# Two ways to apply the causal mask before a row maximum: TensorE for the wide tiles of batch 0 only, VectorE for the narrow ones

## The chip, the cores and the metric

The kernel runs on one core of a Trainium2 chip. The metric is the device time of one execution in microseconds (us); lower is better. The engines of the core are named as the profile names them: PE is TensorE (PEld its weight loads), DVE is VectorE, ACT is ScalarE, POOL is GpSimd, SP is SyncE, which here issues DMAs.

## The reference, cut to what matters

```python
x = L0_attn_x                                    # [2, 1024, 512] float32
xn = layernorm(x)
q, k, v = proj(Wq), proj(Wk), proj(Wv)           # 16 heads of 32
scores = einsum('bhqd,bhkd->bhqk', q, k) / sqrt(32)
scores = where(triu(ones((t, t)), k=1), -inf, scores)
attn = softmax(scores, axis=-1)
s = einsum('bhqk,bhkd->bhqd', attn, v) ... @ Wo.T
hidden = fwht(silu(xn @ W1.T) * (xn @ W3.T))     # 2048 wide
g = silu(hidden @ W2.T)
out = x + s * g
```

The softmax needs the maximum of each row of masked scores before the exponentials. Only that maximum, and the mask in it, is touched here.

## The kernel before

The two batches are worked one after the other. A batch has three stages: `project` (Q, K and V, each product split into high and low parts), `heads` (attention for 16 heads, with the up and gate products of the feed-forward network woven in) and `tail` (attention output, down product, gating, store). In the profiled execution the stage `heads` of batch 0 lies at about 88 to 370 us and that of batch 1 at about 567 to 842 us.

**A head in 12 slots.** `heads` counts slots g; a head has `NS` = 12 of them. In each even slot PE makes the scores of two steps (L1468), ACT takes the exponential (L828), POOL masks the diagonal block in SBUF (L664), ACT makes the high part of the probabilities (L838) and DVE the low part (L1171, called p_lo). PE multiplies them with V in groups (L1486, L1488) and fills every slot with a share of the feed-forward products (L1507), 48 matmuls a head. These masks of POOL and the products of V are not touched.

**The maxima.** Ahead of each head, during the head before it, PE computes for each of the 8 row tiles t the scores of that tile as query rows by keys (L1449), into one of two PSUM places: bank pair `M` for t of 4 to 7 (640 to 1024 columns, two matmuls) and bank `X` for t of 0 to 3 (128 to 512 columns, one matmul). The order is `MAX_ORDER = [7, 0, 5, 1, 6, 2, 4, 3]`, so the two places alternate; item r of this order waits on PE until DVE has done item r-2 (`after(pe, max_done, n * NT + r - 1)`, L1442). The slots are `MAX_AT = [-3, -2, -1, 0, 1, 3, 4, 5]`, counted from the start of the head before, so the first three fall into the last three slots of the head before that. The plan of the slots is written out by hand; no cost model places them.

**The mask in the maxima.** There are two forms, chosen by `masked_by_matmul`:

- by PE: after the scores of a tile, one more matmul (L1452) adds `causal`, -1e38 above the diagonal, to the diagonal 128 x 128 block in PSUM through an identity in bfloat16 (accumulating, `start=False`). DVE then takes a plain row maximum (`tensor_reduce`, L1156).
- by DVE: no extra matmul. DVE takes `tensor_tensor_reduce` (L1158), which adds the mask from SBUF, writes the sum back to the PSUM place and keeps the maximum. It shows as two records in the profile, CUSTOM_DVE_ANT_0 and DVE_READ_ACCUMULATOR2_ANT; the second writes the maximum to `mx`.

Before the change the heads n = 1 to 15 (batch 0 but its first head) go by PE for all 8 tiles; head 0 and all 16 heads of batch 1 go by DVE.

**What follows the maxima.** In slot 7 PE transposes the 8 maxima of the next head (L1458, into bank `X`), having waited for all of them. ACT copies the high part (L877), DVE makes the low part m_lo (L1164), SP stores both by DMA into two rows of the stacked Q tile (L514), and PE's scores of the next head wait for that DMA at their first step (`pe.wait_ge(m_in, (n + 1) * 32)`, ahead of L1468). After every second transpose in batch 0 two small matmuls (L1431) sum squares of weights.

**Order around it.** Each engine works its own list in order. In a slot DVE does first the maximum planned for the slot before, then p_lo, then the reciprocal (L1189), the gating of the feed-forward product (L1193, L1200) and m_lo. Batch 0 has work that batch 1 has not: squares of weights on ACT (L863), their scales on DVE (L1074 to L1084), and slabs of a transform on POOL (L650).

```python
def max_parts(t):
    half = (t + 1) * P // 2
    if t >= TPC:
        return M[:].rearrange("p b w -> p (b w)")[:, W - half:W + half], [(0, half), (half, 2 * half)]
    return X[:, 0, 0:(t + 1) * P], [(0, (t + 1) * P)]
...
for g in range(SLOTS + DRAIN):
    ...
    for jm, r in MAX_PLAN.get(g, []):
        maxima(n0 + jm, r)
```

Of the kernel before, what the change touches and what calls it, by code (L numbers as in the profile page):

```python
# [32 lines left out]
NH, DH = 16, 32  # L33
# [5 lines left out]
TPC = W // P  # L39
# [70 lines left out]
def build(nc, x, wq, wk, wv, wo, w1w3, w2, hadamard, out):  # L110
# [6 lines left out]
    with ctx:  # L117
# [172 lines left out]
        def after(e, s, count):  # L290

            if count > 0:
                e.wait_ge(s, count)
# [55 lines left out]
# [4 lines that stand above are left out]
                return M[:].rearrange("p b w -> p (b w)")[:, W - half:W + half], [(0, half), (half, 2 * half)]  # L353
            return X[:, 0, 0:(t + 1) * P], [(0, (t + 1) * P)]

        def masked_by_matmul(n):

            return 0 < n < NH

        def ct_bank(t):  # L360

# [11 lines left out]
        def stacks_loaded(n):  # L373

            b, j = divmod(n, NH)
            return (b * len(range(j % 3, NH, 3)) + j // 3 + 1) * STACK_LOADS
# [609 lines left out]
        def _(dve):  # L986
# [100 lines left out]
            def project(b):  # L1087
# [40 lines left out]
                for t in range(NT):  # L1128
                    heads_of = lambda v: v.rearrange("p (h d) -> p h d", h=NH)
                    for r in MAX_BEFORE.get(t, []):  # L1130
                        maxima(b * NH, r)
                    g = NQK + t
                    dve.wait_ge(proj_hi_done, b * NG + g + 1)
                    dve.tensor_tensor(vparts[:, t, :, DH:2 * DH], heads_of(group_bank(g)), vparts[:, t, :, 0:DH],
                                      ALU.subtract).then_inc(proj_lo_done, 1)
                    if b == 0 and t == 0:
                        scale_of_w13(0)
                    if t in ONES_AFTER:
                        dve.memset(k_st[ONES_AFTER.index(t)][STACK:STACK + 2, :].bitcast(F32), 1.0
                                   ).then_inc(ones_ready, 1)  # L1140
                    if t == MT_BEFORE - 1:
                        maxima_lo(b * NH)
                        if b == 0:
                            scale_of_w13(1)
                for r in range(FIRST_MAX_AT.count(None)):
                    maxima(b * NH + 1, r)

            def maxima(n, r):

                t = MAX_ORDER[r]  # L1150
                width = (t + 1) * P
                dve.wait_ge(max_ps, n * NT + r + 1)
                dve.sem_inc(max_begun, 1)
                bank, _ = max_parts(t)
                if masked_by_matmul(n):
                    dve.tensor_reduce(mx[n % 2][:, t:t + 1], bank, axis=AX.X, op=ALU.max).then_inc(max_done, 1)  # L1156
                    return
                dve.tensor_tensor_reduce(out=bank, in0=bank,  # L1158
                                         in1=causal[:, S - width:S], scale=1.0, scalar=LOWEST, op0=ALU.add,
                                         op1=ALU.max, accum_out=mx[n % 2][:, t:t + 1]).then_inc(max_done, 1)  # L1160
# [42 lines left out]
            def heads(b):  # L1203
                n0 = b * NH
                for g in range(SLOTS + DRAIN):
                    j, s = divmod(g, NS)
                    for jm, r in MAX_PLAN.get(g - 1, []):
                        maxima(n0 + jm, r)
                    if 1 <= g <= SLOTS:
                        probs_lo(n0 * NS + g - 1)  # L1210
                    if s == COPY_AT[0] and j < NH:
                        denominators(n0 + j, 0)
                    if s == COPY_AT[1] and j > 0:
                        denominators(n0 + j - 1, 1)
                    for jf, c, m in GROUP_PLAN.get(g - 1, []):
                        if m == 0:
                            gate(n0 + jf, c)
                        else:
                            hide(n0 + jf, c)
                    if g - 1 in WO_PLAN:  # L1220
                        split_wo(b, WO_PLAN[g - 1])
                    if g - 1 in MT_PLAN:
                        maxima_lo(n0 + MT_PLAN[g - 1])
                        if b == 0 and MT_PLAN[g - 1] - 1 in SUM_PLAN:
                            scale_of_w13(SUM_PLAN[MT_PLAN[g - 1] - 1])
                    if 0 <= g - SLOTS - CT_AT - 1 < 2:
                        ct_low(b, g - SLOTS - CT_AT - 1)
# [81 lines left out]
        def _(pe):  # L1309
# [21 lines left out]
            def project(b):  # L1331
# [54 lines left out]
                for g in range(2, NG):  # L1386
                    if g - NQK in MAX_BEFORE:
                        pe.wait_ge(proj_lo_done, b * NG + NQK)
                        pe.wait_ge(unscale_done, 1)
                        for r in MAX_BEFORE[g - NQK]:  # L1390
                            maxima(b * NH, r)
                    if g - NQK == MT_BEFORE:
                        transpose_maxima(b * NH)
                        if b == 0:
                            sum_of_squares(1)
                    group(g)
                    for t in XT_AFTER.get(g, ()):
                        transpose_xn(b, t)
                    if b == 0 and g == BOUND_AFTER:
                        bound_of_v()  # L1400
                    if b == 0 and g == 3 * KT:
                        transpose_v_scale()
                    if b == 0 and g == NQK:
                        pe.wait_ge(proj_lo_done, NQK - 1)
                        sum_of_squares(0)
                for r in range(FIRST_MAX_AT.count(None)):
                    maxima(b * NH + 1, r)
# [26 lines left out]
            def maxima(n, r):  # L1434

                t, q, k = MAX_ORDER[r], q_st[n % NH % 3], k_st[n % NH % 3]
                if r == 0:
                    pe.wait_ge(stack_in[n % NH % 3], stacks_loaded(n))
                if r == 1:
                    after(pe, m_lo_done, n)  # L1440
                else:
                    after(pe, max_done, n * NT + r - 1)  # L1442
                if r == 1 and n == 0:
                    pe.wait_ge(w13_scale_step, 1)
                if r == 1 and n - 2 in SUM_PLAN:
                    pe.wait_ge(w13_scale_step, 5 * SUM_PLAN[n - 2] + 1)
                bank, parts = max_parts(t) if t else (X[:, 0, 0:2 * P], [(0, 2 * P)])
                for at, end in parts:
                    mm = pe.matmul(bank[:, at:end], q[0:STACK, t * P:(t + 1) * P], k[0:STACK, at:end],  # L1449
                                   start=True, stop=True)  # L1450
                if masked_by_matmul(n):
                    mm = pe.matmul(bank[:, t * P:(t + 1) * P], ident_b[:], causal[:, S - P:S], start=False, stop=True,  # L1452
                                   skip_group_check=True)
                mm.then_inc(max_ps, 1)
# [56 lines left out]
            def heads(b):  # L1511
# [11 lines left out]
                for g in range(SLOTS + DRAIN):  # L1523
                    if g < SLOTS and g % 2 == 0:
                        scores(n0 * NS + g)
                        scores(n0 * NS + g + 1)
                    at = ffn_upto(g - 1)
                    kept = 1 if (g in CTX_PLAN or b == 0 and g in MAX_PLAN) and g < SLOTS else 0
                    some_ffn(at, ffn_upto(g) - kept)
                    for jm, r in MAX_PLAN.get(g, []):  # L1530
                        maxima(n0 + jm, r)
                    for first, end in CTX_PLAN.get(g, []):
                        for q in range(first, end):
                            context(n0 * NS + q)
                    if g in MT_PLAN:
                        transpose_maxima(n0 + MT_PLAN[g])
                        if b == 0 and MT_PLAN[g] - 1 in SUM_PLAN:
                            sum_of_squares(SUM_PLAN[MT_PLAN[g] - 1])
                    some_ffn(ffn_upto(g) - kept, ffn_upto(g))
                    if g == SLOTS + CT_AT:  # L1540
                        pe.wait_ge(ctx_done, (n0 + NH - 1) * NC + 1)
                        pe.wait_ge(max_done, (n0 + NH) * NT)
                        pe.wait_ge(m_lo_done, n0 + NH)
                        for t in range(2):
                            transpose_ctx(b, t)
# [108 lines left out]
```

## Time and profile before

| | before |
|---|---|
| median of 3 runs | 961.11 us (960.15 to 961.2) |
| own time of the profiled execution | 961.16 us |
| its span, first to last instruction | 959.4 us |
| mean granted TensorE clock | 0.998 |
| PE busy | 945.9 us, 99% |
| DVE busy | 728.7 us, 76% |
| ACT busy | 615.9 us, 64% |
| POOL busy | 340.6 us, 36% |

The profile is one execution seen by the hardware profiler. The engine lines give the busy time and its share of the span. Matmuls overlap in the records (a matmul of 512 columns shows some 0.38 us, though the next one starts 0.22 us later), so for PE the distance from start to start is what counts, not the length of a record. "Idle before" names how long an engine had nothing to do ahead of a record and what it then waited for.

### The profile page before, as it was taken

The numbers are of one execution on the slowest core, as the hardware profiler recorded it, in microseconds if no ns is written. First come the engines' busy times: TensorE is split into PE (matmuls) and PEld (weight loads), VectorE is DVE, ScalarE is ACT, GpSimd is POOL, SyncE is SP. The second block draws the span as 40 slices with busy tenths as digits, with TensorE's granted clock in tenths as the row PEclk, the third lists the DMA queues.
The fourth block names the chain that finished last, engine by engine and source line by source line (L and its number), as shares of the span: only waits on it lengthen the run. The fifth ranks groups of instructions, "written<-read, shape, count | busy, mean of one in ns | idle before, by whom it ended". The sixth has DMA issues, their size and how long they took to land. (4 is left out here: it accounts for less than half of the span.)

```text
span 959.4 us, 18986 instructions
## 1 busy us (share of the span) xinstructions
PE 945.9 (99%) x6528; PEld 661.6 (69%) x6528; DVE 728.7 (76%) x1377; ACT 615.9 (64%) x1316; POOL 340.6 (36%) x590
## 2 busy tenths in 40 slices
PE   8999999999999999999999999999999999999997
PEld 7787666666665666888888866666666666578886
DVE  7977998998998988736655579989899898833343
ACT  4445888888888877723344348787887878832221
POOL 1896663665564442000000114344344443500000
PEclk9999999999999999999999999999999999999999
DMA  9796345543342414961126622323323231181111
GB/s 290 250 279 204 83 118 155 137 113 107 100 114 76 119 27 144 350 242 45 66 95 243 200 56 78 90 57 93 75 77 91 57 85 51 45 359 36 45 44 44
DMA packets 57920, 118.48 MB, mean 123 GB/s; under 512 B 5600, under 2 KB 22624, under 8 KB 57312
## 3 DMA queue, kind: packets, MB, share of 16 engines
q1 hardware_dynamic: 57824, 117.27, 40.6%
q8 instruction: 52, 0.85, 0.4%
q14 instruction: 44, 0.36, 0.1%
HBM read 83.43 MB, written 33.55 MB: 122 GB/s over the span
## 5 line engine op out<-in xcount | busy, mean ns | idle before, releaser
L1171 DVE TENSOR_TENSOR p_lo<-stages,p_hi 128x512 f16<-128x512 f32 (+2 forms) x288 | 199.6, 702 | 27.4 <-ACT p_hi L838 26.3
L1507 PE MATMUL f<-x_hi,w_lo 128*128 128x512 f16 x512 | 195.7, 382 | 0.0
L1507 PE MATMUL f<-x_hi,w_hi 128*128 128x512 f16 x512 | 194.6, 380 | 0.0
L1507 PE MATMUL f<-x_lo,w_hi 128*128 128x512 f16 x512 | 194.4, 380 | 0.0
L828 ACT ACTIVATE stages<-s 128x512 f32<-128x512 f32 (+2 forms) x288 | 150.4, 523 | 65.1 <-PE s L1468 63.1
L838 ACT ACTIVATE p_hi<-stages 128x512 f16<-128x512 f32 (+2 forms) x288 | 160.3, 557 | 25.5 <-POOL stages L664 17.6
L1468 PE MATMUL s<-qk_st 98*128 98x512 f32 (+2 forms) x384 | 129.4, 415 | 2.1 <-DMA qk_st<-m_lo 1.1
L664 POOL TENSOR_SCALAR_AFFINE_SELECT stages<-stages 128x128 f32<-128x128 f32 x192 | 61.0, 324 | 173.3 <-ACT stages L828 172.5
L672 POOL TENSOR_TENSOR w_lo<-w,w_hi 128x256 f16<-128x256 f32 x128 | 95.5, 774 | 55.5 <-ACT w_hi L870 53.1
L1238 DVE TENSOR_TENSOR h_lo<-hidden,h_hi 128x1024 fp32r<-128x1024 f32 x32 | 39.2, 1224 | 84.6 <-ACT h_hi L921 84.6
L921 ACT ACTIVATE h_hi<-hidden 128x1024 fp32r<-128x1024 f32 x32 | 34.0, 1061 | 105.4 <-PE f L1315 105.4
L1313 PE MATMUL f<-g_hi,h_hi 128*128 128x512 f32 x256 | 99.7, 389 | 0.0
L1315 PE MATMUL f<-g_hi,h_lo 128*128 128x512 f32 x256 | 99.6, 389 | 0.0
L1314 PE MATMUL f<-g_lo,h_hi 128*128 128x512 f32 x256 | 99.6, 389 | 0.0
L1449 PE MATMUL m<-qk_st 96*128 96x512 f32 (+3 forms) x256 | 92.2, 442 | 0.0
L1507 PEld LDWEIGHTS f<-x_hi,w_lo 128*128 128x128 f16 x512 | 50.1, 98 | 52.4 <-issue 15.3
L1486 PE MATMUL o<-vparts,p_hi 128*128 128x65 f16 x1152 | 82.7, 193 | 0.0
L1488 PE MATMUL o<-vparts,p_lo 128*128 128x65 f16 x1152 | 82.5, 193 | 0.0
L1468 PEld LDWEIGHTS s<-qk_st 98*128 98x128 f32 x384 | 72.6, 190 | 14.4 <-ACT stages L828 2.7
L1486 PEld LDWEIGHTS o<-vparts,p_hi 128*128 128x128 f16 x1152 | 75.1, 97 | 9.6 <-issue 2.8
L1507 PEld LDWEIGHTS f<-x_lo,w_hi 128*128 128x128 f16 x512 | 50.3, 98 | 44.0 <-issue 6.5
L1507 PEld LDWEIGHTS f<-x_hi,w_hi 128*128 128x128 f16 x512 | 50.9, 99 | 39.6 <-issue 8.8
(208 smaller groups left out, 2055.6 us busy)
## 6 DMA issues: line engine op xcount, KB each, us to landing
qk_st<-qk_parts SPq DMA_DIRECT2D x96, 256.0 KB, 4.4
w<-w1w SPq DMA_DIRECT2D x32, 512.0 KB, 3.6
qk_parts<-qk_hi SPq DMA_DIRECT2D x32, 256.0 KB, 3.4
qk_parts<-qk_lo SPq DMA_DIRECT2D x32, 256.0 KB, 4.6
scan<-w1w SPq DMA_DIRECT2D x12, 512.0 KB, 5.5
wht_in<-w SPq DMA_DIRECT2D x4, 1024.0 KB, 10.7
w_butterflied<-wht_in SPq DMA_DIRECT2D x4, 1024.0 KB, 6.0
w_transformed<-g_hi SPq DMA_DIRECT2D x8, 512.0 KB, 3.3
```

The source lines that it names most:

```text
L672: pool.tensor_tensor(w13_lo[n % 2][at], w13[at], w13_hi[n % 2][at], ALU.subtract).then_inc(w13_lo_done, 1)
L828: act.activation(expd[q % NE][:, 0:end - need], SB[q % 2][:, 0, need - start:end - start], ACT.Exp).then_inc(exp_done, 1)
L838: act.activation(p_hi[s][:], expd[q % NE][:, 0:end - need], ACT.Copy).then_inc(p_hi_done, 1)
L1171: dve.tensor_tensor(p_lo[s][:], expd[q % NE][:, 0:end - need], p_hi[s][:], ALU.subtract).then_inc(p_lo_done, 1)
L1313: pe.matmul(o, a_hi, b_hi, start=first, stop=False)
L1314: pe.matmul(o, a_hi, b_lo, start=False, stop=False)
L1315: return pe.matmul(o, a_lo, b_hi, start=False, stop=last)
L1449: mm = pe.matmul(bank[:, at:end], q[0:STACK, t * P:(t + 1) * P], k[0:STACK, at:end], start=True, stop=True)
L1468: pe.matmul(SB[q % 2][:, 0, 0:end - start], k_st[n % NH % 3][0:STACK + 2, k * P:(k + 1) * P], q_st[n % NH % 3][0:STACK + 2, start:end], st ...
L1486: pe.matmul(o, p_hi[s][:, at:at + P], v, start=k == 0 and t == c * TPC, stop=False, skip_group_check=True)
L1488: mm = pe.matmul(o, p_lo[s][:, at:at + P], v, start=False, stop=t == k, skip_group_check=True)
L1507: mm = pe.matmul(F[m][:, 0, :], w, v, start=k == 0, stop=k == GMM - 1)
```

## The change

The choice of the form depends on the tile too: PE masks only the tiles t of 4 to 7 (`TPC` is 4), and the tiles 0 to 3 of the heads 1 to 15 take the DVE form. In the order of the maxima these are the items r = 1, 3, 5 and 7. Order, slots, waits and buffers stay.

```diff
-        def masked_by_matmul(n):
+        def masked_by_matmul(n, t):
 
-            return 0 < n < NH
+            return 0 < n < NH and t >= TPC
...
                 bank, _ = max_parts(t)
-                if masked_by_matmul(n):
+                if masked_by_matmul(n, t):
                     dve.tensor_reduce(mx[n % 2][:, t:t + 1], bank, axis=AX.X, op=ALU.max).then_inc(max_done, 1)
                     return
                 dve.tensor_tensor_reduce(out=bank, in0=bank,
...
-                if masked_by_matmul(n):
+                if masked_by_matmul(n, t):
                     mm = pe.matmul(bank[:, t * P:(t + 1) * P], ident_b[:], causal[:, S - P:S], start=False, stop=True,
                                    skip_group_check=True)
                 mm.then_inc(max_ps, 1)
```

## Rows read from the trace of the kernel before

**Rows 1.** The page: busy us of an engine (share) xinstructions; granted clock in 40 slices.

```profile
PE 945.9 (99%) x6528; PEld 661.6 (69%) x6528; DVE 728.7 (76%) x1377; ACT 615.9 (64%) x1316; POOL 340.6 (36%) x590
...
PEclk9999999999999999999999999999999999999999
```

**Rows 2.** Busy us in the middle of both `heads` stages: PE, PEld, DVE, ACT, POOL, clock, DMA.

```profile
118.00:350.00 232.00, 231.08 (x1992) 141.50 (x1989) 206.94 (x381) 197.11 (x451) 128.56 (x229) 1.00 0.41 108
600.00:820.00 220.00, 219.84 (x1851) 136.34 (x1847) 199.52 (x449) 180.75 (x422) 96.32 (x203) 1.00 0.29 74
```

**Rows 3.** Waits of PE, whole span, longest first in part: us in total, times, longest.

```profile
PE f L1329 <- POOL causal L620: 3.1, 1, 3.1
PE s L1468 <- DMA qk_st<-m_lo: 1.1, 2, 0.9
PE s L1468 <- ACT stages L828: 1.0, 2, 0.5
```

**Rows 4.** Line L1452, the masks of PE: duration ns min/median/max, first and last start.

```profile
L1452 PE MATMUL xs<-causal,ident_b x60: 230/230/233, 87.7 to 348.1; 128*128 128x128 bf16 x60
```

**Rows 5.** Timeline of PE, batch 0, tile 1: start us, length, engine, line, operation.

```profile
214.93 0.47 PE L1449 MATMUL xs<-qk_st 96*128 96x256 f32 x1
215.24 0.23 PE L1452 MATMUL xs<-causal,ident_b 128*128 128x128 bf16 x1
215.30 0.38 PE L1507 MATMUL f<-x_hi,w_lo 128*128 128x512 f16 x1
```

**Rows 6.** Timeline of PE, batch 1, the same place, tile 1.

```profile
706.67 0.47 PE L1449 MATMUL xs<-qk_st 96*128 96x256 f32 x1
706.98 0.39 PE L1507 MATMUL f<-x_hi,w_hi 128*128 128x512 f16 x1
```

**Rows 7.** Timeline of PE: transposes of the maxima in batch 0, then in batch 1.

```profile
153.92 0.27 PE L1458 MATMUL xs<-ident,mx 128*8 128x128 f32 x1
...
171.65 0.27 PE L1458 MATMUL xs<-ident,mx 128*8 128x128 f32 x1
...
225.18 0.27 PE L1458 MATMUL xs<-ident,mx 128*8 128x128 f32 x1
...
681.93 0.27 PE L1458 MATMUL xs<-ident,mx 128*8 128x128 f32 x1
...
699.13 0.27 PE L1458 MATMUL xs<-ident,mx 128*8 128x128 f32 x1
...
716.42 0.27 PE L1458 MATMUL xs<-ident,mx 128*8 128x128 f32 x1
```

**Rows 8.** Groups by form of DVE, 700 to 820 us: count, busy us, mean ns, idle.

```profile
L1158 DVE DVE_READ_ACCUMULATOR2_ANT mx<- 128x1 f32 x56 | 7.8, 139 | 0.0
```

**Rows 9.** Timeline of DVE around tile 3, batch 0 then batch 1; in brackets idle before.

```profile
219.82 0.42 DVE L1171 TENSOR_TENSOR p_lo<-stages,p_hi 128x256 f16<-128x256 f32 x1 [0.79 <-ACT p_hi L838]
...
221.30 0.29 DVE L1171 TENSOR_TENSOR p_lo<-expd,p_hi 128x128 f16<-128x128 f32 x1 [0.59 <-ACT p_hi L838]
...
223.90 0.68 DVE L1156 TENSOR_REDUCE mx<-xs 128x1 f32<-128x512 f32 x1
...
224.50 1.18 DVE L1171 TENSOR_TENSOR p_lo<-stages,p_hi 128x512 f16<-128x512 f32 x1
...
715.35 0.69 DVE L1158 CUSTOM_DVE_ANT_0 xs<-xs,causal 128x512 f32<-128x512 f32 x1
...
715.96 0.14 DVE L1158 DVE_READ_ACCUMULATOR2_ANT mx<- 128x1 f32 x1
715.96 1.18 DVE L1171 TENSOR_TENSOR p_lo<-stages,p_hi 128x512 f16<-128x512 f32 x1
```

**Rows 10.** Timeline: issue of the m_lo DMA, then the next head's first scores, twice.

```profile
211.25 0.64 SPq L514 DMA_DIRECT2D qk_st<-m_lo  x1
...
213.86 0.75 PE L1468 MATMUL s<-qk_st 98*128 98x512 f32 x2
...
300.20 0.64 SPq L514 DMA_DIRECT2D qk_st<-m_lo  x1
...
304.10 0.67 PE L1468 MATMUL s<-qk_st 98*128 98x512 f32 x2 [0.92 <-DMA qk_st<-m_lo]
```

## The prediction, made before the change was run

> **What bounds the kernel now.** I read the page first [rows 1]: PE is busy for 945.9 us, 99% of the span, at a granted clock of 0.9 or more in every slice (the upper of its two levels, 2.4 GHz), and DVE for 76%. Busy records of PE overlap, so the next view is the table of stretches [rows 2]. In the middle of the `heads` stage of batch 0, where the change acts, PE is busy for 231.08 of 232 us and DVE for 206.94; in the same part of batch 1, which already takes every maximum in the DVE form, PE is busy for 219.84 of 220 us and DVE for 199.52. Third are the waits of PE [rows 3]: outside the start of the program the longest is 1.1 us in total, on the DMA of m_lo. So PE is the bound all through the `heads` stages: what PE no longer issues there comes off the end, as long as nobody makes PE wait instead. The question is thus what a mask costs PE from start to start, and how far DVE is from making PE late.
>
> **The terms of the sum.**
>
> *Taken off PE.* The masks that write bank X are 60, four for each of the heads 1 to 15, all of one size, 230 ns long in the record [rows 4]. That length is no price, since matmuls overlap. The price is in the timeline. In batch 0 the scores of tile 1 start at 214.93, the mask at 215.24 and the next product at 215.30 [rows 5]: 0.37 us from scores to product, of which the mask holds 0.06. In batch 1 the same scores go straight to the same product, 706.67 to 706.98, 0.31 us [rows 6]. The difference is 0.06 to 0.07 us with the rounding of the starts. This comparison also holds the change of number format from the scores to the 16-bit product, which stays without the mask: it costs nothing more. A second way to the same price is the length of a whole head, from one transpose of maxima to the next: 17.73 us in batch 0 (153.92 to 171.65, an interval without the two extra matmuls of L1431) and 17.20 and 17.29 us in two heads of batch 1 (681.93 to 699.13 to 716.42) [rows 7]. The 0.53 and 0.44 us between them are eight masks, less whatever differs otherwise: 0.066 and 0.055 each. So the ends of the range are 0.055 and 0.070 us a mask: 60 x 0.055 = 3.3 and 60 x 0.070 = 4.2 us. I take 0.066, where the direct pair and the shorter of the two heads meet; the lower end rests on a head length that also holds another order of the feed-forward products. That gives 60 x 0.066 = 4.0 us.
>
> The Trainium skill, page "TensorE: Matmul & The Clock Gate", section "Back-to-back issue gap", gives two other prices for a 128-column matmul at the full clock: about 81 ns in a sustained stream in which each has its own weight load, and about 56 ns for the matmul alone. By the first the sum would be an estimated 60 x 0.081 = 4.9 us, by the second 3.4 us. The pair in this trace lies between the two, and I stay with it.
>
> *Put on DVE.* Sixty plain maxima become masked ones. The widest, 512 columns: the plain one starts at 223.90 and the p_lo behind it at 224.50, 0.60 us; the masked one starts at 715.35 and the p_lo behind it at 715.96, 0.61 us [rows 9]. The second record, 139 ns on average [rows 8], lies in that row beside the p_lo, which starts at the same moment. So what comes behind the maximum on DVE is late by 0.01 us at the low end; at the high end, if the second record were paid in full, by 0.15. That is 0.04 to 0.6 us a head. I take the low end, because the row shows exactly this pair of instructions. The result itself, and so the semaphore for PE, comes later by the second record: 0.61 + 0.14 = 0.75 us from the start in place of 0.68.
>
> *What hides it.* DVE needs 206.94 us in 232 us of batch 0. With 17.78 us a head (232 us are 13.05 heads) that is 15.9 us a head, 1.9 idle. After the change a head lasts 17.5 us on PE and DVE needs 15.9 to 16.5, so 1.0 to 1.6 us stay idle; batch 1, with 199.52 of 220 us, runs with 1.6 idle a head of 17.24 and PE does not wait. The cover is the idle time ahead of p_lo, 0.79 and 0.59 us in the head around 220 us [rows 9], where DVE waits for ACT: delay of the items r = 1, 3 and 5 dies there. If it were gone, up to 0.6 us a head would pass on.
>
> *The waits behind the masked maxima.* PE's item r waits for item r-2, and PE's transpose waits for item 7. The latter is the tightest: item 7 ends at 223.90 + 0.68 = 224.58 and the transpose starts at 225.18, 0.60 us of room; in batch 1 item 7 ends at 715.96 + 0.14 = 716.10 and the transpose starts at 716.42, 0.32 us of room, still no wait [rows 7, 9]. The change takes 0.07 from the room by the later result and 0.07 by the mask that PE no longer has in between, so 0.46 stays. Queued behind the transpose on PE are all feed-forward products and the scores of the next head, and for its result wait ACT, DVE's m_lo and SP's DMA.
>
> *The DMA behind the transpose.* From the issue of m_lo to the next head's first scores are 2.61 us in a usual head (211.25 to 213.86), and once 3.90 us, with PE idle for 0.92 (300.20 to 304.10) [rows 10]. Between transpose and first scores lies one removed mask, tile 0, 0.07 us. I cost it at nothing, as batch 1 has three masks fewer in that place and the waits of PE on this DMA are two in the whole run, 1.1 us together [rows 3].
>
> *Not moved.* POOL and SP get no instruction more or fewer; their work is released by the heads' pace and shifts with it. Head 0 and batch 1 keep their code. ACT has 197.11 of 232 us, 2.7 idle a head, enough for a head that is 0.27 (4.0 / 15) shorter. The PSUM place X is now written by DVE too, but its next user waits for the same semaphore as before.
>
> **The sum.** 961.16 us, the profiled execution's own time (its span of 959.4 and 1.8 around it), less 4.0 gives 957.2. The median of the runs shown, 961.11, lies 0.05 below that execution, so the forecast for the median is 957.1 us.
>
> **The rivals.**
>
> *DVE passes its delay on.* If every masked maximum holds DVE for 0.15 us more and the idle time ahead of p_lo does not take it up, the transpose's room is 0.60 - 0.60 - 0.14 = -0.14 us, and each of 15 heads gives back 0.14, 2.1 us in all: 959.2 us. For it speaks DVE's load of 89% before; against it that the p_lo of batch 1 starts with the second record and that batch 1 has only half that room without a wait. The Trainium skill, page "VectorE: DVE Perf Modes", speaks for it: by the section "Two Vector instructions with no wait between them" an operation with an accumulator output is two instructions, and by "Rules for kernel authors" a flush is paid for each, so that the count of operations is what to save. Our row of tile 3 does not agree. I give it 6%.
>
> *The gain is met by a wait, nothing comes out.* PE reaches some release of ACT, POOL or DMA sooner and waits there for as long as it saved: 961.1 us. PE's waits on ACT of 1.0 us in total are all there is of it, and batch 1 shows that heads of 17.3 us can be had. 3%.
>
> *Slower: the m_lo DMA is late in more heads.* The place is the first scores of a head. The price of one late landing is 3.90 - 2.61 = 1.3 us. It decides from the point at which more than three of the 15 heads (4.0 / 1.3) are late in addition to the one that is now; with five it would be 961.1 - 4.0 + 6.5 = 963.6 us. For it: the DMA ran late once in batch 0, and a later m_lo or another pace shifts it against the loads behind it. Against it: all other heads of batch 0 and the shorter ones of batch 1. 4%.
>
> *The change does not act.* Both users of the condition, on PE and on DVE, take it with the tile, so the counts must change; under 1%, with the time of before.
>
> **How the numbers follow.** The forecast, 957.1 us, has 87%. Its own spread: 4.2 in place of 4.0, and the late DMA of batch 0 gone, gives 955.6; another 0.3 for the runs' own scatter (theirs before was about 1 us from lowest to highest) gives 955.3. At the other end 3.3 and one more late DMA give 959.1, which also reaches the DVE rival. The range is 955.3 to 959.1. A measurement of this kernel can tell about 0.2% from no change, 1.9 us, so "faster" is anything below 959.2: nearly all of the forecast's case and half of the DVE rival, 0.91. "Same" is the rest of that rival and the case without gain, 0.06; "slower" 0.03.
>
> **What would show it.** Right: the 60 records of L1452 on xs gone and 60 more masked maxima on xs in their place; heads without L1431 of 17.45 to 17.50 us (17.73 less 0.27) from transpose to transpose; scores of a narrow tile followed by the product after 0.31 us; waits of PE in the stage as before. Wrong: an idle record of PE ahead of the transpose or of the scores, named DVE mx or DMA m_lo, in most heads; p_lo starting 0.14 us after the second record's start in place of with it; or the same waits with heads that got shorter by less than 0.2 us, which would mean that the masks had been hidden under something.

## The result and the profile after

The changed kernel takes 965.25 us (median of 6 runs, 963.73 to 966.73) against 961.15 us before (6 runs of the same comparison). The ratio is 1.0037, with a 95% interval of 1.002 to 1.0054: slower by 4.1 us, where the forecast was faster by 4.0. The profiled execution took 965.63 us, its span 963.9. Of the kernel before, one execution in the first group of the experiments ran at a granted clock of 0.557 and took 1603.59 us; it is left out of every median and ratio here.

The page of the changed kernel, busy us of the engines:

```profile
PE 945.5 (98%) x6468; PEld 656.7 (68%) x6468; DVE 741.3 (77%) x1437; ACT 616.5 (64%) x1316; POOL 338.4 (35%) x590
```

PE has the 60 matmuls fewer (6468 for 6528), but its busy time is only 0.4 us less in a span that is 4.5 us longer. DVE has 60 records more and 12.6 us more to do [rows 1].

The middle of both `heads` stages, as in [rows 2]:

```profile
118.00:350.00 232.00, 227.71 (x1923) 136.34 (x1920) 215.73 (x427) 195.03 (x447) 123.44 (x225) 1.00 0.40 108
600.00:820.00 220.00, 218.72 (x1839) 135.35 (x1838) 198.56 (x444) 178.66 (x417) 94.53 (x201) 1.00 0.29 75
```

In batch 0 PE is now idle for 4.3 of 232 us, where it was 0.9, and DVE is busy for 8.8 us more. Batch 1, whose code is the same, is nearly as before in this stretch; its 1.1 us more of idle PE are one late DMA of m_lo and small waits like it.

The waits of PE over the whole span, to be read beside [rows 3]:

```profile
PE f L1507 <- DVE hidden L1200: 4.5, 10, 1.1
PE f L1329 <- POOL causal L620: 3.1, 1, 3.1
PE s L1468 <- DMA qk_st<-m_lo: 1.3, 2, 1.1
```

The first line is new. PE waits for the gating of a feed-forward product (L1200, called hide below), not for a maximum and not for the DMA. So DVE is late at hide, which was none of the places that I had watched. What makes it late is in the groups of DVE by form, 118 to 350 us; first the kernel before:

```profile
L1171 DVE TENSOR_TENSOR p_lo<-stages,p_hi 128x384 f16<-128x384 f32 x26 | 18.9, 726 | 0.1
...
L1171 DVE TENSOR_TENSOR p_lo<-stages,p_hi 128x256 f16<-128x256 f32 x26 | 10.8, 417 | 10.4 <-ACT p_hi L838 10.4
```

and the same two groups in the changed kernel:

```profile
L1171 DVE TENSOR_TENSOR p_lo<-stages,p_hi 128x256 f16<-128x256 f32 x26 | 22.3, 857 | 6.2 <-ACT p_hi L838 6.2
L1171 DVE TENSOR_TENSOR p_lo<-stages,p_hi 128x384 f16<-128x384 f32 x26 | 19.0, 730 | 0.1
```

Nobody touched p_lo, yet its form of 256 columns costs 11.5 us more in this stretch, 857 ns for one in place of 417. That mean hides two kinds: 16 of the 26 have their old 0.42 us, and 10, one for each head of this stretch with two slab steps, last 1.55 us (10 x 1.14 = 11.4). The timeline shows why. In the kernel before, DVE and POOL at the end of a head:

```profile
212.83 0.75 DVE L1171 TENSOR_TENSOR p_lo<-stages,p_hi 128x384 f16<-128x384 f32 x1
213.12 0.61 POOL L664 TENSOR_SCALAR_AFFINE_SELECT expd<-expd 128x128 f32<-128x128 f32 x1
213.51 0.28 DVE L1156 TENSOR_REDUCE mx<-xs 128x1 f32<-128x128 f32 x1
213.71 1.55 POOL L650 TENSOR_TENSOR wht_in<-wht_in 128x512 f32<-128x512 f32 x1
213.71 0.41 DVE L1171 TENSOR_TENSOR p_lo<-stages,p_hi 128x256 f16<-128x256 f32 x1
214.04 0.74 DVE L1200 SCALAR_TENSOR_TENSOR hidden<-hidden,w_unscale,f 128x512 f32<-128x512 f32 x1
```

and the same place of the changed kernel, with PE's wait:

```profile
214.72 0.76 DVE L1171 TENSOR_TENSOR p_lo<-stages,p_hi 128x384 f16<-128x384 f32 x1
215.01 0.61 POOL L664 TENSOR_SCALAR_AFFINE_SELECT expd<-expd 128x128 f32<-128x128 f32 x1
...
215.40 0.29 DVE L1158 CUSTOM_DVE_ANT_0 xs<-xs,causal 128x128 f32<-128x128 f32 x1
215.59 1.28 POOL L650 TENSOR_TENSOR wht_in<-wht_in 128x512 f32<-128x512 f32 x1
215.60 0.13 DVE L1158 DVE_READ_ACCUMULATOR2_ANT mx<- 128x1 f32 x1
215.60 1.55 DVE L1171 TENSOR_TENSOR p_lo<-stages,p_hi 128x256 f16<-128x256 f32 x1
...
217.08 0.73 DVE L1200 SCALAR_TENSOR_TENSOR hidden<-hidden,w_unscale,f 128x512 f32<-128x512 f32 x1
...
217.87 0.39 PE L1507 MATMUL f<-x_hi,w_hi 128*128 128x512 f16 x1 [0.39 <-DVE hidden L1200]
```

Two instructions start at the same moment, p_lo of 256 columns on DVE and a slab step of a transform on POOL (L650). Both read two tensors in SBUF. One of them runs at its own length, and the other lasts longer by most of the first. Before, p_lo has 0.41 us and the slab step 1.55, which is 0.28 more than its own 1.27; after, the slab step has 1.28 and p_lo 1.55, which is 1.14 more than its own 0.41. Both times the record grows by 0.13 to 0.14 us less than the length of the other's record. The start of the slab step lies within 2 ns of that of p_lo in all 11 heads of the kernel before that have it, and p_lo is the one that isn't delayed in all 11; in the changed kernel the slab step starts 7 to 9 ns ahead, and p_lo is the delayed one in all 11. The difference comes from the instruction in front: from the start of the maximum of tile 0 to that of p_lo are 200 to 201 ns with the plain form and 208 to 210 with the DVE form. Before, POOL lost 0.28 us that nobody needed. Now DVE loses 1.14 us, and PE stands behind hide.

That the coincidence is so exact in every head has a likely reason in the same rows, though I didn't test it: POOL's mask of 128 columns lasts 0.61 us, against 0.29 elsewhere, as if it had lost in the same way to the p_lo of 384 columns. So both engines would be set off by the same event, and only the length of one short instruction on each side would decide.

The Trainium skill, page "SBUF — State Buffer", section "Who interferes with whom", states this: DVE's second pair of ports into SBUF is shared with GpSimd and works as an exclusive lock, a DVE instruction with two SBUF inputs contends there with a GpSimd instruction that reads SBUF, and the order of issue decides which of the two is blocked. These rows agree: the same two instructions lengthen each other by 0.28 or by 1.14 us, by which of them goes first.

Transposes of the maxima on PE, to be read beside [rows 7]. The interval 155.16 to 172.67 has no slab step, the next two do:

```profile
155.16 0.27 PE L1458 MATMUL xs<-ident,mx 128*8 128x128 f32 x1
172.67 0.27 PE L1458 MATMUL xs<-ident,mx 128*8 128x128 f32 x1
191.08 0.27 PE L1458 MATMUL xs<-ident,mx 128*8 128x128 f32 x1
209.22 0.27 PE L1458 MATMUL xs<-ident,mx 128*8 128x128 f32 x1
```

Without one a head has 17.51 us for 17.73 before: here the change does what it was forecast to do. With slab steps most heads have 18.1 to 18.4 us for 17.7 to 17.9 before (the 18.41 us from 172.67 to 191.08 include 0.3 us of a late DMA). One, from 118.04 to 136.87, has 18.83: hide had only 0.2 us of room there before, and PE now waits 1.1 us for it.

The two waits on m_lo in the list of waits above both lie in batch 1, where the kernel before had one of 0.2 us. They cost more than their own length, as two transposes of the maxima in batch 1 show, the first pair from the kernel before, the second from the changed one:

```profile
630.16 0.27 PE L1458 MATMUL xs<-ident,mx 128*8 128x128 f32 x1
647.38 0.27 PE L1458 MATMUL xs<-ident,mx 128*8 128x128 f32 x1
...
632.40 0.27 PE L1458 MATMUL xs<-ident,mx 128*8 128x128 f32 x1
650.95 0.27 PE L1458 MATMUL xs<-ident,mx 128*8 128x128 f32 x1
```

This head has 18.55 us for 17.22. From the first to the last transpose batch 1 lasts 1.9 us longer than before, batch 0 3.2 us (270.29 for 267.12), and the part ahead of them is 0.5 us shorter: together, to the rounding, the 4.5 us between the two spans. What set the DMA late in batch 1 was not looked for. The same head has 18.57, 18.66 and 18.13 us in three of the kernels below (the other order on DVE, the changed kernel with POOL held back, the memset on POOL) and 17.22 to 17.25 in all the others.

### The profile page after: what moved, and what is told of

The parts are those of the page before. It is cut to its first block and busy times, and to the rows that moved or that the text cites. A ratio compares the mean times of both kernels' runs of the same rounds, so it can differ in the third digit from the quotient of the medians.

```text
span 963.9 us, 18926 instructions
## 1 busy us (share of the span) xinstructions
PE 945.5 (98%) x6468; PEld 656.7 (68%) x6468; DVE 741.3 (77%) x1437; ACT 616.5 (64%) x1316; POOL 338.4 (35%) x590
## 5 line engine op out<-in xcount | busy, mean ns | idle before, releaser
L1171 DVE TENSOR_TENSOR p_lo<-stages,p_hi 128x512 f16<-128x512 f32 (+2 forms) x288 | 212.2, 746 | 21.2 <-ACT p_hi L838 20.8
L838 ACT ACTIVATE p_hi<-stages 128x512 f16<-128x512 f32 (+2 forms) x288 | 160.4, 557 | 25.8 <-POOL stages L664 17.7
```

Of the source, the lines that this page charges most:

```text
L838: act.activation(p_hi[s][:], expd[q % NE][:, 0:end - need], ACT.Copy).then_inc(p_hi_done, 1)
L1171: dve.tensor_tensor(p_lo[s][:], expd[q % NE][:, 0:end - need], p_hi[s][:], ALU.subtract).then_inc(p_lo_done, 1)
```

## The experiments

Two theories stood against each other. **Race**: p_lo of 256 columns loses to a slab step of POOL because the DVE form of tile 0 makes it 10 ns late; the load of DVE does not matter. **Load**: DVE simply has too much to do in batch 0 once it masks as well. The runs came in three groups; each is compared with the kernel before on the same chip (medians 960.7, 960.3 and 960.91 us).

### The suspected tile alone, and all but it

```diff
 # e1_tile0
-            return 0 < n < NH and t >= TPC
+            return 0 < n < NH and t > 0
 # e2_tiles123
-            return 0 < n < NH and t >= TPC
+            return 0 < n < NH and (t >= TPC or t == 0)
```

> Only tile 0 (item r = 1, 128 columns) of heads 1 to 15 takes the DVE form; the other seven tiles stay with PE. Two theories. Race: in the 11 heads that have two slab steps on POOL, DVE's p_lo of 256 columns (third last step of the head before) starts within 0.01 us of POOL's second slab step (L650); the DVE form of tile 0 makes it some 0.01 us late, the slab step goes first, p_lo lasts 1.55 us in place of 0.41 and hide (L1200) makes PE wait ahead of a feed-forward product. Then this kernel has nearly the whole loss of the change: PE waits on L1200 of 4 to 5 us over some 10 heads, about 0.6 us a head lost in 11 heads with the wait behind it, less 15 x 0.066 = 1.0 us: 966 to 967 us. Load: DVE is late because it has more to do in the stage; one quarter of the change then has at most a quarter of the effect, no wait of PE on L1200, and 960 to 962 us.

Measured: 967.69 us, ratio 1.0065 (1.0044 to 1.0086). One quarter of the change loses more than the whole. The wait is there:

```profile
PE f L1507 <- DVE hidden L1200: 3.9, 11, 0.9
```

> Tiles 1, 2 and 3 of heads 1 to 15 take the DVE form, tile 0 stays with PE. Race: the instruction in front of the critical p_lo is the plain maximum again, p_lo of 256 columns lasts 0.41 us, no wait of PE on L1200, and the saving is 45 x 0.066 = 3.0 us: 958.1 us. Load: three quarters of the extra work are there, so at least half of the loss of the change should remain: 963 to 965 us.

Measured: 957.73 us, ratio 0.9966 (0.995 to 0.9982), and p_lo at its old length:

```profile
L1171 DVE TENSOR_TENSOR p_lo<-stages,p_hi 128x256 f16<-128x256 f32 x26 | 10.9, 418 | 9.7 <-ACT p_hi L838 9.7
```

Three quarters of the work that was added to DVE cost nothing, and the kernel gains 3.0 us. Load falls with this pair.

### The lateness without the change

The kernel before, with one small memset behind the maximum of tile 0. It writes a spare column and touches no mask.

```diff
                 if masked_by_matmul(n):
                     dve.tensor_reduce(mx[n % 2][:, t:t + 1], bank, axis=AX.X, op=ALU.max).then_inc(max_done, 1)
+                    if t == 0:
+                        dve.memset(room[:, 0:1], 0.0)
                     return
```

> The kernel before, every mask in its old form, with one memset of 128 x 1 on DVE behind the maximum of tile 0 in heads 1 to 15, so that p_lo starts 0.02 to 0.06 us later. Race: the slab step of POOL goes first in the 11 heads that have one, p_lo of 256 columns lasts 1.5 us, PE waits on L1200 (a little less than in the changed kernel, as PE itself is not earlier): 965 to 968 us. Load: 15 x 0.06 = 0.9 us more on an engine that is idle for 1.9 us a head changes nothing: 961 us.

Measured: 967.77 us, ratio 1.0069 (1.0046 to 1.0092). Its timeline (in this kernel p_lo is L1173 and hide L1202):

```profile
217.58 0.28 DVE L1156 TENSOR_REDUCE mx<-xs 128x1 f32<-128x128 f32 x1
217.78 1.27 POOL L650 TENSOR_TENSOR wht_in<-wht_in 128x512 f32<-128x512 f32 x1
217.79 1.55 DVE L1173 TENSOR_TENSOR p_lo<-stages,p_hi 128x256 f16<-128x256 f32 x1
217.81 0.06 DVE L1158 MEMSET room_before_o<- 128x1 f32 x1
```

The memset itself is 0.06 us long and lies beside p_lo; what it moved is the start of p_lo, to 209 ns behind the start of the maximum in place of 201, and that is enough to turn the order in all 11 heads. Fifteen such instructions, 0.9 us of work by their records, go with 7.1 us in the medians. Some 5.5 us of them are the 11 heads, most of which last 0.5 us longer; the profiled execution also has 3.0 us of waits on the DMA of m_lo, so the rest isn't shown to be p_lo's.

### The change with POOL held back

```diff
                         mask(n * NS + s)
+                        if s == NS - 1 and n < LAST_SLAB_AT + 8:
+                            pool.wait_ge(p_lo_done, n * NS + s)
```

> The change as it is, and POOL waits for the p_lo of 256 columns (semaphore p_lo_done) before the second slab step of a head, so that this p_lo cannot lose. Race: p_lo of 256 columns lasts 0.41 us, slab steps 1.27 us, no wait of PE on L1200, and the full 4.0 us of the forecast come out: 957.1 us, within 956 to 958.5. Load: DVE has the same work as in the changed kernel, so its time stays at 963 to 966 us.

Measured: 959.15 us, ratio 0.9974 (0.996 to 0.9988). That is 6.1 us under the changed kernel by the medians and under the one before, though 0.65 us above the range that I had given.

```profile
214.41 0.29 DVE L1160 CUSTOM_DVE_ANT_0 xs<-xs,causal 128x128 f32<-128x128 f32 x1
214.62 0.14 DVE L1160 DVE_READ_ACCUMULATOR2_ANT mx<- 128x1 f32 x1
214.62 0.41 DVE L1173 TENSOR_TENSOR p_lo<-stages,p_hi 128x256 f16<-128x256 f32 x1
214.96 0.73 DVE L1202 SCALAR_TENSOR_TENSOR hidden<-hidden,w_unscale,f 128x512 f32<-128x512 f32 x1
215.12 1.28 POOL L650 TENSOR_TENSOR wht_in<-wht_in 128x512 f32<-128x512 f32 x1 [0.48 <-DVE p_lo L1173]
```

POOL waits for 0.48 us, both instructions have their own length, and the heads have 17.50 and 17.65 us in turn, the second kind with the sums of squares. All of DVE's instructions of the changed kernel are here; only the order against POOL differs. Two heads of batch 0 fall out of this: one of 18.67 us, with a wait of 0.8 on a DMA of Q, and one of 18.37, whose loss the waits do not name. One place of the projections has a wait of 1.7 us, for 0.5 before, and batch 1 has its late head, with a wait of 1.2 on m_lo. So the time of this execution, 960.58 us, says less than its heads.

> The kernel before with the wait of POOL for the p_lo of 256 columns ahead of the second slab step. Race: this p_lo wins there anyway, so nothing changes: 960 to 962 us; the gain of the same wait in the changed kernel is then not a merit of the wait by itself. Rival: the wait frees POOL or DVE of something else and gains in both kernels alike, 959 us or less.

Measured: 961.21 us, ratio 1.001 (0.9995 to 1.0025). The same wait is worth nothing where p_lo does not lose.

### Next to nothing on POOL to lose to

```diff
 # in slab_step, for both e7_after_slim (changed kernel) and e8_before_slim (kernel before)
+                if s == 3 or (s == 2 and st >= 2):
+                    o, a, c = o[..., 0:1], a[..., 0:1], c[..., 0:1]
                 pool.tensor_tensor(o, a, c, ALU.subtract if half else ALU.add).then_inc(wht_step, 1)
```

> The changed kernel with the slab steps that lie in the heads of batch 0 (L650, the last stages of slab 2 and all of slab 3) cut to the last column; this leaves out a part of the transform of W2. Race: POOL has nothing long to hold against p_lo, so p_lo of 256 columns lasts 0.41 us in every head, no wait of PE on L1200, heads of 17.5 us, and the time is 4.0 us under that of the kernel before with the same cut. Load: DVE's own work is unchanged, so the loss against that kernel stays at 3 to 5 us.

> The kernel before with the same cut of the slab steps. In the kernel before no wait of PE came from them, so both theories expect 960 to 961.5 us, with p_lo of 384 columns at 0.56 us in every head in place of 1.26 in every second. The difference to the changed kernel with the same cut is what decides: race -4.0 us, load +3 to +5 us.

Measured: 957.68 us (ratio 0.9977, 0.9968 to 0.9987) and 960.53 us (1.0005, 0.9991 to 1.0019). The difference is -2.85 us by the medians: the sign of the race theory, less than its 4.0. Head by head the change is worth 0.22 to 0.24 us: 17.64 and 17.49 us (transposes at 241.43, 259.07 and 276.56) against 17.88 and 17.71 us (243.38, 261.26 and 278.97). Four masks a head, so 0.056 us a mask and not 0.066.

The cut did not take the meeting away. In six heads a cut step still starts beside p_lo, here 1 to 3 ns ahead of it, and p_lo goes first all the same, so that this time the step is the longer one, 0.48 us for 0.19 (changed kernel with the cut):

```profile
229.35 0.48 POOL L652 TENSOR_TENSOR wht_in<-wht_in 128x2 f32<-128x2 f32 x1
229.36 0.42 DVE L1173 TENSOR_TENSOR p_lo<-stages,p_hi 128x256 f16<-128x256 f32 x1
```

### Another order on DVE

```diff
+                    late = b == 0 and s == NS - 1
-                    for jm, r in MAX_PLAN.get(g - 1, []):
+                    for jm, r in () if late else MAX_PLAN.get(g - 1, []):
                         maxima(n0 + jm, r)
                     if 1 <= g <= SLOTS:
                         probs_lo(n0 * NS + g - 1)
+                    for jm, r in MAX_PLAN.get(g - 1, []) if late else ():
+                        maxima(n0 + jm, r)
```

> The changed kernel with one swap on DVE in batch 0: in the last slot of a head p_lo of 256 columns comes before the maximum of tile 0, not behind it. Race: this p_lo starts some 0.2 us earlier, right at the end of the p_lo of 384 columns, well ahead of POOL's slab step, so it cannot lose to it; at worst POOL's mask of 128 columns (0.29 us) goes first. No wait of PE on L1200, heads of 17.5 to 17.65 us, 957 to 959 us. Rival (the DVE form itself slows the p_lo behind it, or the load): another order of the same instructions changes little, 964 to 966 us.

Measured: 958.36 us, ratio 0.9972 (0.9954 to 0.9989). p_lo of 256 columns now starts 0.2 us ahead of the slab step, and the slab step loses (1.44 us). The mean of 462 ns for p_lo is no sign of a loss: right behind the p_lo of 384 columns it has 0.51 us, also in a head without a slab step. So the cure needs no wait: p_lo must only start clearly ahead.

### No mask on PE at all

> All eight tiles of heads 1 to 15 take the DVE form (no mask of PE at all), with POOL's wait for p_lo ahead of the second slab step. Race theory with the mask's price of 0.066 us: 120 x 0.066 = 7.9 us less than before, 953 us, heads of 17.2 us as in batch 1, if no other pair of DVE and POOL instructions comes out the other way round; if one does, 956 to 962 us with a p_lo longer than its usual length and a wait of PE on DVE behind it. Load: DVE has still more to do than in the changed kernel, 966 us or more.

> All eight tiles of heads 1 to 15 in the DVE form, without POOL's wait. Race: tile 0 is the DVE form as in the changed kernel, so p_lo of 256 columns loses in the 11 heads with slab steps and PE waits on DVE; against the changed kernel 60 more masks are gone from PE, which it meets as a longer wait, so 964 to 966 us, against 956.2 us with POOL's wait. Rival: the wait did nothing and the kernel of 956 us owes its time to the missing masks alone; then this one has 956 us too.

> PE masks tile 0 alone, DVE the other seven tiles of heads 1 to 15, no wait of POOL. Race: the instruction in front of the critical p_lo is the plain maximum, so p_lo of 256 columns keeps its 0.41 us, no wait of PE on L1200. By the head lengths seen so far a mask is worth 0.056 us: 105 x 0.056 = 5.9 us less than before, 955 us, if the 0.02 us that the wide maxima add bring no other pair into the wrong order; with some waits behind the wide maxima 956 to 958 us. Load: 966 us or more.

The edits are the condition alone (`return False`, with and without POOL's wait; `t == 0`). Measured: 956.18 us with the wait (ratio 0.9952, 0.993 to 0.9974), 963.64 us without it (1.0025, 1.0011 to 1.004), and 957.03 us with PE on tile 0 alone (0.9951, 0.9932 to 0.9971). The same 120 masks are moved in the first two, and 7.5 us lie between their medians, 7.0 by the ratios, since the two ran on different chips: p_lo against the slab step again, as the waits of PE from 118 to 350 us of the kernel without the wait show:

```profile
PE f L1507 <- DVE hidden L1200: 5.0, 9, 1.1
```

I had expected 953, 964 to 966 and 955 us. The first misses by 3.2: with 120 x 0.056 = 6.7 us it should have been near 954 on that day's 960.3, and its heads with slab steps have 17.4 to 17.6 us, not the 17.3 and 17.45 of its heads without. No wait of PE is named there, so that 0.1 us a head stays unexplained. The second, 963.64, lies just under its range. The third lies 2.0 above the 955, though in the trace its heads of batch 0 came out as forecast: from the first to the last transpose of batch 0 are 260.77 us for 267.12 before, 6.3 us less, with p_lo at 0.41 us in every one of the 11 heads, and in batch 1 1.5 us more, two late DMAs of m_lo. Still, both are faster than either kernel, and the intervals of the two overlap, so which of them is better is open.

### What of POOL's work blocks

```diff
+                if s == 3 or (s == 2 and st >= 2):
+                    pool.memset(o, 0.0).then_inc(wht_step, 1)
+                    return
                 pool.tensor_tensor(o, a, c, ALU.subtract if half else ALU.add).then_inc(wht_step, 1)
```

> The changed kernel with the slab steps in the heads of batch 0 replaced by a memset on POOL of the same output, which writes SBUF and reads nothing; this leaves out a part of the transform of W2. If what p_lo loses to is POOL's reading of SBUF (p_lo reads two tensors there), p_lo of 256 columns lasts 0.41 us beside the memset, and the time is 957 to 959 us. If any use of SBUF by POOL blocks it, p_lo is longer by what is left of the memset when it starts. A memset may be shorter than the 1.27 us of the step, so the overlap in the timeline decides, not the time alone.

Measured: 958.2 us, ratio 0.9966 (0.9951 to 0.998). The overlap (p_lo is L1174 here):

```profile
211.17 0.52 POOL L651 MEMSET wht_in<- 128x512 f32 x1
211.42 0.54 DVE L1174 TENSOR_TENSOR p_lo<-stages,p_hi 128x384 f16<-128x384 f32 x1
...
212.09 0.41 DVE L1174 TENSOR_TENSOR p_lo<-stages,p_hi 128x256 f16<-128x256 f32 x1
```

In this head the memset is over before the p_lo of 256 columns begins. But the p_lo of 384 columns starts 0.25 us into the memset and keeps its 0.54 us, where the slab step in that place made it 0.75 us in heads of this kind and 1.26 in the others. And in six other heads the memset meets the p_lo of 256 columns itself, 24 to 26 ns ahead of it, where a slab step 7 ns ahead was enough to block it:

```profile
193.83 0.52 POOL L651 MEMSET wht_in<- 128x512 f32 x1
193.86 0.14 DVE L1161 DVE_READ_ACCUMULATOR2_ANT mx<- 128x1 f32 x1
193.86 0.42 DVE L1174 TENSOR_TENSOR p_lo<-stages,p_hi 128x256 f16<-128x256 f32 x1
```

It keeps its 0.42 us in all six. A write alone did not block it. The page of the skill named above says the same, contention with what reads SBUF and not with what only writes it, and these overlaps agree.

## Why the prediction was wrong

**What PE bounds.** Right. In the heads without a slab step the time is what PE issues, before and after.

**The mask's price.** Right in kind, too high in size: 0.056 us and not 0.066, so 60 masks are worth 3.4 us, not 4.0. The pair of [rows 5, 6] is right about the stretch (the same scores still have 0.31 us without a mask), but the head as a whole gets shorter by less, 0.22 us for four. The value at the low end, taken from the head's length, was the better one; I had set it aside.

**DVE's extra work.** The term itself was right: what comes behind a masked maximum is late by 0.01 us, and the second record lies beside it. The step that failed is the next one, "what hides it": I set DVE's lateness against its idle time per head and found that 0.01 us can't matter. Idle time covers a delay only if the delay stays as long as it is. Here 0.01 us turned into 1.14 us, because it changed which of two engines goes first.

**The waits watched.** The transpose of the maxima kept 0.40 us or more of room in batch 0, near what was worked out (0.46). The DMA of m_lo was late twice, as before, but both times in batch 1, where it stands behind the 1.9 us by which that stage is longer; the rival that gave this DMA more late landings thus has a share in the span, in a place that it did not name and with no run that ties it to the change. Both rivals with a wait on DVE or on this DMA had the wrong place for the loss of batch 0: the wait was hide's, for which I never worked out the room. It was 0.74 to 0.84 us in most heads before; p_lo's 1.14 us and the earlier PE used it up and made that product 0.46 to 0.55 us late, and the head loses some 0.1 us more around the fifth maximum.

**"POOL: not moved".** This sentence is where the cause should have been found. POOL gets no other instruction, but here its slab steps were touched by a shift of DVE by 8 ns. The rows were in the trace of the kernel before: a slab step of 1.55 us where others have 1.27, starting in the same hundredth as a p_lo, in front of it exactly the instruction that the change replaces. Batch 1, on which I leaned for "no wait with the DVE form", has no slab steps, and so could not show it.

**The sum as it came out.** 60 x 0.056 = 3.4 us gained; 11 heads with a slab step that lose 0.62 to 0.65 us each against the same heads of the kernel with POOL's wait (18.30 and 18.12 for 17.65 and 17.50), some 7.0 us. Net +3.6 us, all of it in batch 0, where the profiles show +3.2 between the first and the last transpose. The medians say +4.1 and the spans +4.5. That these lie so near is in part luck, since the spans hold 1.9 us of batch 1 and 0.5 less ahead of the heads, which the sum does not have. The named wait of 4.5 us is less than the 7.0, since records of matmuls overlap and the idle time between them is shorter than the time that the next start is late (0.39 and 0.55 us in the head at 217.87).

## What to carry to other kernels

A shift of a few nanoseconds is harmless only where no two engines reach for the same thing at that moment. Before costing an edit on DVE at nothing, look on the timeline for GpSimd instructions that start together with a DVE instruction of two SBUF inputs and for lengths above the usual of the same form; each such pair is a coin that any edit ahead of it can turn, and the price is most of the length of the instruction that goes first (1.14 us beside one of 1.28 here). Where one side has nobody waiting for it, put it behind the other by a semaphore or by order, rather than trust to the order that came out by itself.

## What was not expected of the hardware

The outcome is as sharp as it could be: with the slab step within 2 ns of p_lo, p_lo is never the one delayed in 11 heads; with the step 7 to 9 ns ahead, it always is. It repeats in every kernel run here that keeps the slab steps whole and the order on DVE: 0.41 us in the two kernels that keep the plain maximum in front of p_lo (the one with tiles 1 to 3, the one with PE on tile 0 alone) as well as in the one before with POOL's wait, 1.53 to 1.55 in the three others with something longer there and no wait (tile 0 alone, the memset, no mask on PE). Over all of them p_lo goes first with the slab step from 2 ns ahead to 4 ns behind, and with the cut step still at 3 ns ahead; it loses from 6 ns ahead on. Being first by the record is thus not quite the same as going first. And the second record of a masked maximum, 139 ns [rows 8], lies beside the next instruction on DVE in all of them; what the DVE form costs there is the 8 ns.
